# Two programs of a transformer kernel merged: a mixture-of-experts FFN issued piece by piece inside a 1024-step recurrence

## What is computed

```python
x = x + 0.5 * _L0_ffn_ref(_layernorm(x), ...)     # first routed FFN
x = x + _L0_attn_ref(_layernorm(x), ...)          # hierarchical attention
x = x + 0.5 * _L0_ffn_ref(_layernorm(x), ...)     # second routed FFN (in the change)
x = x + 0.5 * _L1_ffn_ref(_layernorm(x), ...)     # "a": binarised FFN
x = x + _L1_attn_ref(_layernorm(x), ...)          # "p" and "r": recurrence, then MLP
x = x + 0.5 * _L1_ffn_ref(_layernorm(x), ...)     # "z": binarised FFN again
...
    # routed FFN: small attention over the 4 batch entries, router over 8 experts, top 2
    h_mid = gelu_tanh(einsum('th,ehf->etf', x, moe_w1))      # F = 256
    expert_out = einsum('etf,efh->eth', h_mid, moe_w2)       # all 8 experts, weighted
...
    # recurrence, over T = 1024 steps
    state = tanh(state @ A.T + xb_t)                         # state is [4, 32]
    out = state @ C.T + xd_t
...
    # binarised FFN: W -> mean|W| * sign(W); 128 -> 512 -> 128 with erf-gelu
```

## Time and profile before

| | |
|---|---|
| median of three runs (range) | 2226.37 us (2222.71 to 2226.94) |
| the profiled execution: its time, its span | 2226.66 us, 2224.9 us |
| PE busy / DVE / ACT / POOL, share of the span | 83% / 45% / 39% / 9% |
| TensorE clock granted, mean of the span | 0.735 of full |
| first product of the second routed FFN's experts | 1009.25 us |
| first and last recurrence step | 1345.94 us, 2176.97 us |

### The profile page before, as it was taken

How to read it: one execution, slowest core, us unless ns; L and a number is a source line. 1 busy time by engine, 2 the same in 40 slices (tenths; PEclk the granted TensorE clock), 3 DMA queues, 4 the chain that set the end, 5 groups by cost and what they waited for, 6 DMA issues and landing times. The chain is left out here.

```text
span 2224.9 us, 37410 instructions
## 1 busy us (share of the span) xinstructions
PE 1851.9 (83%) x13672; PEld 1372.4 (62%) x13672; DVE 1009.9 (45%) x3005; ACT 862.7 (39%) x2377; POOL 193.9 (9%) x314
## 2 busy tenths in 40 slices
PE   1889896848858588558898977799999999999886
PEld 1666675447556485546666765576777777766665
DVE  3666754775866778746666642111111111111102
ACT  1434442745546456424353432232323232323231
POOL 1211201001010010012121100000000000000000
PEclk8999996969879799779999985555555555555556
DMA  6000000000000000000000000000000000000000
GB/s 156 1 1 0 0 1 1 2 1 3 2 1 3 2 2 2 1 1 1 1 0 1 1 1 1 1 1 5 1 6 1 5 1 5 1 5 1 5 1 10
DMA packets 12015, 13.03 MB, mean 6 GB/s; under 512 B 1648, under 2 KB 10640, under 8 KB 11280
## 3 DMA queue, kind: packets, MB, share of 16 engines
q1 hardware_dynamic: 11840, 10.77, 1.8%
HBM read 8.67 MB, written 2.10 MB: 5 GB/s over the span
## 5 line engine op out<-in xcount | busy, mean ns | idle before, releaser
L1006 ACT ACTIVATE r_state<-r_scan 32x4 f32<-32x4 f32 x1024 | 166.9, 163 | 592.6 <-PE r_scan L941 589.3
L941 PEld LDWEIGHTS r_scan<-r_state,rnnA 128*32 128x32 f32 x2048 | 186.3, 141 | 253.3 <-issue 153.6
L941 PE MATMUL r_scan<-r_state,rnnA 128*32 128x4 f32 x2048 | 275.4, 205 | 52.1 <-ACT r_state L1006 52.1
L286 PEld LDWEIGHTS f_down<-moe,f_hT 128*128 128x128 f32 x2048 | 251.3, 194 | 56.9 <-issue 54.0
L277 PE MATMUL f_up<-f_x2T,moe 128*128 128x512 f32 x512 | 248.8, 610 | 11.6 <-ACT f_hT L193 11.6
L286 PE MATMUL f_down<-moe,f_hT 128*128 128x128 f32 x2048 | 254.0, 278 | 0.0
L463 DVE SCALAR_TENSOR_TENSOR x_all<-f_down,f_weight,x_all 128x128 f32 (+1 forms) x512 | 144.1, 344 | 166.6 <-PE f_down L286 163.9
L193 ACT ACTIVATE f_hT<-f_up 128x512 f32<-128x512 f32 x256 | 149.9, 598 | 139.0 <-PE f_up L277 137.6
L1618 DVE TENSOR_TENSOR att_big<-at_ring,att_big 128x512 f16<-128x512 f32 x192 | 123.9, 685 | 49.2 <-ACT att_big L1300 48.4
L277 PEld LDWEIGHTS f_up<-f_x2T,moe 128*128 128x128 f32 x512 | 90.5, 195 | 90.0 <-issue 63.5
L1300 ACT ACTIVATE att_big<-at_ring 128x512 f16<-128x512 f32 x192 | 111.4, 596 | 66.5 <-PE at_ring L1433 64.6
(11 more groups left out here) (241 smaller groups left out, 3202.2 us busy)
## 6 DMA issues: line engine op xcount, KB each, us to landing
x_all<-in_x SPq DMA_DIRECT2D x4, 512.0 KB, 6.1
moe<-in_moe SPq DMA_DIRECT2D x2, 1024.0 KB, 7.1
out<-x_all SPq DMA_DIRECT2D x8, 256.0 KB, 2.3
bin<-in_bin SPq DMA_DIRECT2D x2, 256.0 KB, 7.6
mlp<-in_mlp SPq DMA_DIRECT2D x2, 256.0 KB, 6.0
att_big<-in_att_wq SPq DMA_DIRECT2D x1, 512.0 KB, 11.2
att_big<-in_att_wk SPq DMA_DIRECT2D x1, 512.0 KB, 13.2
att_big<-in_att_wv SPq DMA_DIRECT2D x1, 512.0 KB, 14.9
```

Of the source, the lines that this page charges most:

```text
L286: last = nc.tensor.matmul(down[e % 2][:, s * 128:(s + 1) * 128], hT[c % H_RING][:, s * 128:(s + 1) * 128], w2[:, c * 128:(c + 1) * 128], s ...
L941: nc.tensor.matmul(scan[b][0:STATE, NB * t:NB * (t + 1)], rnnA[:, :], last, start=False, stop=(t == 127), skip_group_check=True).then_inc( ...
L1006: nc.scalar.activation(state[b][0:STATE, NB * t:NB * (t + 1)], scan[b][0:STATE, NB * t:NB * (t + 1)], ACT.Tanh).then_inc(s_tanh, 1)
```

## The change

`second` and the second `ffn` become one phase `rest`, a function `routed_ffn_and_recurrence`, without barriers inside. The routed FFN of groups 0 and 1, the binarisation and "a" of group 0 come before the recurrence. The routed FFN of group m = g+2 runs inside the 128 steps of group g; "a" is one group ahead now, "r" one behind, "z" two behind. `slots` deals the pieces of a group out over its 128 steps in proportion to a duration `NS` that each kind is given. Pieces are larger: half of an up product (256 columns, one product), two down products of a routed expert, four down products of a dense FFN, all four transposes of a tile. `plan_of` puts the gelus (512 columns for the experts, 256 for the dense FFNs) behind the tanh of a step after the product they read. PSUM: the recurrence keeps two banks, the experts' up products have two instead of three and down one instead of two, transposes, qkv, projection and router share one bank; the dense FFNs' up products go round over the experts' up and down banks. The loops are unrolled.

```diff
-            SLOTS = {
-                "turn_a": [0, 1, 2, 3], "mix": list(range(4, 12)),
...
+            def up_half(pe, m, c, half, g):
+
+                if half == 0:
+                    pe.wait_ge(s_h, ONE + CHUNKS * m + max(c - 1, 0))
...
+                part = slice(256 * half, 256 * half + 256)
+                ins = nc.tensor.matmul(up[c % 2][:, part], w1[:, c * 128:(c + 1) * 128], x2T[m % 2][:, part],
+                                       start=True, stop=True)
...
+            def down_tile(pe, m, e, s):
+                if s == 0:
+                    pe.wait_ge(s_h, ONE + CHUNKS * m + 2 * e + 2)
+                    pe.wait_ge(s_add, ONE + EXPERTS * m + e)
+                for c in (2 * e, 2 * e + 1):
+                    ins = nc.tensor.matmul(down[:, s * 128:(s + 1) * 128], hT[c % H_RING][:, s * 128:(s + 1) * 128],
...
+            NS = {up_half: 480, down_tile: 500, k_turn_tiles: 1000, p_turn1: 1000, p_turn2: 1000, p_turn3: 1000,
+                  p_qkv: 740, p_proj: 1000, p_router: 500, k_up_half: 480, k_down_tile: 1000, input_product: 900,
+                  mix_tiles: 1000}
...
+            def routed_order(m, g):
+
+                ups = lambda e: [(up_half, (m, c, half, g)) for c in (2 * e, 2 * e + 1) for half in range(2)
+                                 if real(m) and e < EXPERTS]
...
+                for e in range(EXPERTS):
+                    order += ups(e + 1)
+                    if real(m):
+                        order += [(down_tile, (m, e, s)) for s in range(NB)]
+                    order += between(e, m, m + 2, m + 1, g)
+                return order
...
+            def slots(g):
+
+                order = routed_order(g + 2, g) + dense_order(g)
+                total, at, out_ = sum(NS[f] for f, _ in order), 0, []
+                for f, args in order:
+                    out_.append((int(128 * (at + NS[f] / 2) / total), f, args))
+                    at += NS[f]
+                return out_
...
+                p_turn1(pe, 0)
+                for i, b in enumerate((post_misc, pre_misc)):
+                    pe.wait_ge(s_bin, i + 1)
...
+                run(routed_order(-1, -9))
+                run(routed_order(0, -9))
+                order = routed_order(1, -9)
...
+                        if f is down_tile and args[1:] == (EXPERTS - 1, NB - 1):
+                            if real(g + 4):
+                                p.append((at + 1, a_exp, (g + 4,)))
+                            if real(g + 3):
+                                p.append((at + 1, a_gexp, (g + 3,)))
...
-PHASES = ("ffn", "attn", "ffn", "second")
+PHASES = ("ffn", "attn", "rest")
```

More of the change, by code:

```diff
@@ L543, in layouts_second_half @@
     }
[L546 to L594, removed]
@@ L636, in second_half @@
+        sgn = sb("sgn", [128, 2, FC, 128])
+        alpha = sb("alpha", [128, FC + 1])
         scan = [bank(f"scan{i}") for i in range(2)]
[L637 to L640, removed]
+        up, down, turn = [bank(f"up{i}") for i in range(2)], bank("down"), bank("turn")
@@ L641, in second_half @@
+        post_misc, pre_misc = bank("post_misc"), bank("pre_misc")
+        RING = [up[0], up[1], down]
+        FIRST = {"a": 0, "r": FC, "z": 2 * FC}
         W1 = {"a": S["bin1"], "r": S["mlp1"], "z": S["bin1"]}
@@ L706, in v_norm @@
[L706 to L713 removed]
+                        last = dve.bn_aggr(mv[:, s, :], stats[:, s, :])
@@ new lines, in add_expert @@
+                def add_expert(g, e):
+                    dve.wait_ge(s_down, ONE + EXPERTS * g + e + 1)
+                    dve.wait_ge(s_add, ONE + EXPERTS * g + e)
+                    for s in range(NB):
+                        last = dve.scalar_tensor_tensor(grp(g)[:, s, :], down[:, s * 128:(s + 1) * 128],
+                                                        weight[g % 2][:, s, e:e + 1], grp(g)[:, s, :],
+                                                        ALU.mult, ALU.add)
+                    last.then_inc(s_add, 1)
@@ new lines, in bin_weights, with routed @@
+                def bin_weights():
+                    for i, (n, b) in enumerate((("bin1", post_misc), ("bin2", pre_misc))):
+                        dve.wait_ge(s_bturn, i + 1)
+                        dve.tensor_copy(S[n][:, :], b[:, :]).then_inc(s_bready, 1)
+                def routed(m, g):
+                    front, back, own, post = real(m + 2), real(m + 1), real(m), real(g - 1)
+                    if front:
+                        v_stats(m + 2)
+                    if real(g - 2) and g - 2 != GROUPS - 2:
+                        v_nT("z", g - 2)
+                    if own:
+                        add_expert(m, 0)
+                    if back:
+                        v_values(m + 1)
@@ new lines, in routed @@
+                    if own:
+                        add_expert(m, 1)
+                    if back:
+                        v_heads(m + 1)
+                    if own:
+                        add_expert(m, 2)
+                    if front:
+                        v_norm1(m + 2)
+                    if post:
+                        k_norm("r", g - 1, mixed)
+                    if own:
+                        add_expert(m, 3)
+                    if back:
+                        v_after(m + 1)
```

901 lines of the change are left out of this document (656 added, 245 removed).

## The result

The merged kernel takes 2410.81 us (median of 4 runs, 2385.71 to 2423.10) against 2225.97 us of the kernel before on the same chip: ratio 1.0751, 95% interval 1.0695 to 1.0807. It is 7.5% slower. The forecast was 2388 us. The profiled execution took 2422.16 us, with a span of 2420.3 us; the four executions (2422.16, 2423.1, 2385.71 and 2399.47 us) differ by 1.6%, and the shorter ones had more of the upper clock (mean granted clock 0.687, 0.687, 0.702 and 0.695).

What follows compares the result with a forecast made beforehand. PE's own issue order at TensorE's lower clock was taken to set the pace; 1115 us to the first step, 1215 loop and 56 tail made 2386 of span, plus 1.8 around it, 2388 us; range 2080 to 2440.

Steps and rivals of the forecast that it cites:

- the likeliest case: Whole kernel at 1.2 GHz nearly throughout: 2388 us, own range 2340 to 2430, chance 52%.
- The choice of the clock: In the merged loop TensorE was taken to run at 1.2 GHz, not 2.4; a near thing for groups 2 to 5.
- rows 8: Profile rows of the kernel before: clock rose in dense "a" products, fell within 5 us once steps began.
- The first step: Start of the recurrence: first step at 1115 us, 231 us earlier than before; bounds 1100 to 1130.
- The loop: Merged recurrence of eight groups at 1.2 GHz: 1215 us against 831 before, a full group 177 us.
- rows 7: Profile rows giving products in a row 0.12 us a record of 128 columns at 2.4 GHz.
- The table load: ACT's function-table loads in the loop: 1.28 us each, three a group, adding 0.9 us to a step, no extra drain.
- The tail: Work after the last step: 56 us against 47.9 before, as "z" of group 6 joins it.
- 1: Rival: clock holds at 2.4 GHz through group 5; 1978 us, faster by 11%; chance 10%.
- 2: Rival: clock low in groups 0 and 1, 2.4 GHz for most of groups 2 to 5; 2102 us; chance 13%.
- 3: Rival: clock goes up and down, parts of groups 2 to 5 at 2.4 GHz; 2130 to 2330 us; chance 20%.
- Rival 4: 1.2 GHz and late DVE: PE waits for `add_expert` in six groups, 48 us; 2436 us; chance 5%.

Runs made afterwards that it cites:

- every packed version: Kernels with each group's pieces dealt over fewer steps; merged kernel over the first 88 of 128 steps 2211.68 us, over 64 steps 2188.07 us.
- spread stretch: Merged kernel, groups 0 to 5: first fifth of pieces in 10 steps, rest one a step over 93; groups 6 and 7 in 40 and 28 steps; 2190.18 us.
- The best merged version: Merged kernel with pieces packed into the first 72 steps of groups 0 to 5, 40 of group 6, 28 of group 7; 2148.66 us, ratio 0.9693.
- packed in fours: Kernel before the change, slots divided by four: four products a step in the first 32 steps, none in the other 96; 2160.0 us, ratio 0.971.
- The two groups with equal records and different clocks: Groups 1 and 2 of the kernel before with two slots a step; same 360 PE records in 58.1 and 81.7 us; kernel 2203.51 us.

## Why the prediction was right

**Right in kind, and in size within 1%.** 2388 was forecast and 2410.81 measured, inside the range and inside the likeliest case's own range (2340 to 2430). Its sum against the profiled span: 2386 + 11 (start) + 27 (loop) - 3 (tail) = 2421. Part of the closeness is luck: the loop's prices were some 63 us too low, and rises of the clock that the sum doesn't contain gave back some 36 of them (below).

**The choice of the clock** decided the sign, and it held. The step at which I expected the fall, a table load in group 0, is where it fell. My sentence that nothing in the later groups is dense enough for a rise was not quite right: it rose three times, for 51 us. A full group costs 177 us at the low and 104 at the high clock by the prediction's prices, so 51 us at the high clock stand for 87 at the low one and gave back some 36 (an estimate). Of the reason I gave, forty empty steps and waits behind table loads in group 0, the wait is borne out: the clock fell in one. But with the loads gone it fell 34 us later in a wait for a norm, which I had not counted among them; and what the empty steps did to it there no run isolates. I had also read rows 8 too smoothly. The fall in the kernel before came 5.4 us after the first step (1351.36), in bare steps, but 3.7 us before it PE had stood for 1.49 us:

```profile
1347.65 0.30 PE L860 MATMUL r_pre_misc<-ident,r_xn_a 128*128 128x128 f32 x1 [1.49 <-DVE x_all L735]
```

**The first step** came at 1126.0, not 1115. The first expert product was at 1021.5 (predicted 1018; the first 52 us of this stretch ran at a mean clock of 0.58, which I hadn't priced). From there to the step it is 104.5 us against 97. The clock of this stretch was 0.94 in the mean, where the 38.7 us a group came from one at 0.97, and that stands for some 3 of the 7.5 us (an estimate). Experts and "a" of group 0 are interleaved there, and the rest isn't split.

**The loop** took 1241.8 us against 1215. Adding the 36 us that the rises gave back, the prices were 63 us or 5% too low at 1.2 GHz. By group, all at 0.50, they were 8.8, 5.2, 5.7 and 4.0 us low in g = 1, 5, 6 and 7. Where: half an up product or two downs took 1.35 us instead of 1.31 and 1.34, at most 3 us a group. Half of the mix took 3.25 us (step to step), not 2.19, 2 us a group. Its four products, of 32 and of 128 rows in turn, each of two records, started 0.74 to 0.77 us apart:

```profile
1982.46 0.83 PE L1244 MATMUL m_post_misc<-rnnD,m_nT_p 128*128 128x128 f32 x2
...
1983.22 0.83 PE L1242 MATMUL m_post_misc<-rnnC,m_state 32*128 32x128 f32 x2
```

Four products of a dense down, all of 128 rows, took 2.20 us, as priced (2.19). Steps with one qkv piece took 1.97 us against 1.73, and steps with transposes took 1.25 when nothing was late but up to 5.6 when the norm was. The waits other than for a tanh come to 5 us in g = 1, where 2.7 and about 1 were forecast. The prices at 2.4 GHz were low as well, 0.70 us for half an up product where 0.78 was measured: its two records of 256 columns went in at 0.43 us, and by the 0.12 us of rows 7 they are 0.48.

**The table load** itself was 1.28 us in the loop as before, and the gelu followed 0.01 us after it (1128.01 + 1.28 = 1129.29, 1129.30). The forecast counted 18 loads in the loop, three a group; the trace has 17, as the last group with experts has two. The drain that the Trainium skill ("ScalarE: Activation LUTs", What ACT_TABLE_LOAD costs) adds to each load is not seen. But 0.9 us a load was too little as well: without the loads the kernel was some 54 us faster by the ratios (1.0751 to 1.0507; 74 us by the medians), since the clock fell later and rose more often.

**The tail** took 52.6 us, 56 predicted.

**Rivals.** 1 and 2 did not occur. 3, the clock going up and down, occurred in a weak form (three rises) and is what every packed version does. Rival 4 is refuted: it wanted 48 us of waits for `add_expert`, and in the loop there was one, of 1.1 us; all waits for DVE were 18. The advice of the Trainium skill ("TensorE: Matmul & The Clock Gate", Why this matters for your kernels), no PE idle gap between bursts, is not enough here: from 1805.7 to 2159.9 PE never stood longer than 1.2 us and its records cover 95% (336.58 of 354.2 us), and the clock stayed at 1.2 GHz; in one spread stretch they cover 92% (74.13 of 80.8 us) and the clock was 2.4 GHz.

**What the merge is worth.** By my ledger it costs 384 us in the loop for 231 outside at the low clock; measured, 411 for 220. The best merged version, 2148.66 us, stands against 2160.0 for the kernel before with its pieces packed in fours, on the same chip. That is 0.5%, and each ratio (0.9693 and 0.971) lies in the interval of the other (0.9618 to 0.9768, and 0.9688 to 0.9732). So nearly all of the 3.1% by which the best version beats the kernel before is had without the merge, and these runs don't show the merge itself to be worth anything. Packings of the kernel before beyond four were not tried.

**What stays open.** What exactly makes the clock rise or hold. The two groups with equal records and different clocks, and the spread stretch that ran at 1.00 in group 5 and at 0.72 in group 3, which had more records in the same steps, say that it isn't the mean density of a stretch alone. Several falls lie in or just behind a wait of PE of 1 to 2 us (1129.8, and 1501.9, where it had stood for 1.64 us for a norm), but others don't (1549.7), so where in the stream the dense runs and the pauses lie may count as well. No run here isolates that. Nor did any run take out a wait for a norm.

## What to carry to other kernels

Where a serial chain of small steps leaves room for other work, don't deal the work out evenly: price the loop at both clocks first (here 0.78 and 1.35 us for the same step), and put the pieces together so that PE runs in dense stretches and the bare chain alone. Before two programs are merged, try on the old one what the merge's order brings, since the gain may come from the packing alone. And where a function table changes in such a loop, look at what follows the wait in the clock row, not only at the load's 1.28 us.

## What the runs showed of the hardware that was not expected

- Work that is thrown away made a kernel faster: 256 further products of 256 columns, 2411 to 2300 us (ratio 1.0751 to 1.0304), with the clock of group 2 at 0.86 and 0.78 instead of 0.65 and 0.52.
- A busy PE is no sign of the upper clock: records covering 95% of 173 us at 0.50, 92% of 80.8 us at 1.00.
- One wait of PE of 1.07 us behind a table load stood at a fall of the clock that then lasted 348 us; without the load the loop kept it for 38 us, up to a wait of 1.64 us.
- Products of two records, of 32 and of 128 rows in turn, cost 0.76 us each at 1.2 GHz, where those of equal rows cost 0.43 (2 x 0.2125). The two also differ in what they multiply, and no run changed one thing alone.
